# Pre-activation convolution with binarised inputs on one core: fills first, shorter warm-up, both x copies ahead of the signs, and a new order on VectorE

## The reference

```python
mean, std = jnp.mean(W), jnp.sqrt(jnp.var(W))
B = jnp.sign(W[None] - mean + us[:, None, None, None, None] * std)   # 5 sign filters
alpha = jnp.linalg.solve(Bf.T @ Bf, Bf.T @ wf)
W_eff = jnp.einsum('m,mhwio->hwio', alpha, B)
...
for n in range(3):
    An = jnp.sign(jnp.clip(X + v[n], 0.0, 1.0) - 0.5)
    out = out + beta[n] * (conv(An) + sum_alpha * bias[n])
...
x = x + conv_ref(group_norm(x))     # G = 32 groups: one channel each
```

## Time and profile before

| | |
|---|---|
| median of 3 runs | 214.75 us (213.79 to 215.58) |
| profiled execution | 215.01 us |
| its span | 213.2 us |
| busy: PE, DVE, ACT, POOL | 82%, 79%, 66%, 29% |

### The profile page before, as it was taken

One profiled execution on the slowest core, in us unless ns is written; L12 is line 12 of the kernel. 1 busy time (PEld: TensorE's weight loads), 2 busy tenths in 40 slices (PEclk: granted clock), 3 DMA queues, 4 the chain that ended last, 5 costly groups with the idle time before them and its releaser, 6 DMA issues.

```text
span 213.2 us, 4788 instructions
## 1 busy us (share of the span) xinstructions
PE 175.3 (82%) x1812; PEld 132.9 (62%) x1812; DVE 168.5 (79%) x422; ACT 139.9 (66%) x183; POOL 61.4 (29%) x76
## 2 busy tenths in 40 slices
PE   1675128969999999999999999999999998889771
PEld 0574018658777676767777676767676765657451
DVE  4369989478989898989898989888888989874141
ACT  2639157078787878787878787878787878673120
POOL 1279023313223323232323232323232323240000
PEclk9999999979999999999999999999999999999996
DMA  4899123032697978788798879879897455658524
GB/s 117 241 271 272 36 58 101 0 89 70 177 246 221 251 200 233 220 224 261 188 279 238 227 198 267 258 205 246 220 242 221 124 167 144 164 160 226 156 65 151
DMA packets 21030, 39.61 MB, mean 186 GB/s; under 512 B 9744, under 2 KB 9744, under 8 KB 21008
## 3 DMA queue, kind: packets, MB, share of 16 engines
q1 hardware_dynamic: 20272, 39.27, 66.7%
q10 hardware_dynamic: 736, 0.04, 0.2%
HBM read 13.15 MB, written 12.85 MB: 122 GB/s over the span
## 4 chain that ended last, share of the span: by engine, by line
DVE 46%; ACT 21%; issue 13%; PE 11%; DMA 5%; SPq 2%; DVEq 0%; ACTq 0%
DVE y_nat L546 9%; ACT signs L348 8%; DVE s_even L612 8%; DVE raw_stats L555 7%; ACT y_ch L361 6%; ACT x_ch L343 4%; PE conv_ps L722 4%; DVE neg_thr L591 4%; DVE hi_part L601 4%; DVE hi_part L599 4%; DMA x_nat<-in_x 3%; ACT root L353 2%; PE x_ps L684 2%; PE y_ps L757 2%; DVE lane_stats L562 2%
## 5 line engine op out<-in xcount | busy, mean ns | idle before, releaser
L722 PE MATMUL conv_ps<-s_even,w_mm 128*64 128x448 f16 (+1 forms) x576 | 104.7, 336 | 2.4 <-DMA s_odd<-s_even 2.4
L725 PE MATMUL conv_ps<-s_odd,w_mm 128*64 128x448 f16 (+2 forms) x576 | 104.6, 324 | 0.0
L348 ACT ACTIVATE signs<-x_ch,neg_thr 128x784 f16<-128x784 f32 x96 | 85.4, 941 | 20.5 <-DVE neg_thr L591 20.5
L722 PEld LDWEIGHTS conv_ps<-s_even,w_mm 128*64 128x64 f16 x576 | 61.3, 111 | 30.1 <-issue 4.3
L725 PEld LDWEIGHTS conv_ps<-s_odd,w_mm 128*64 128x64 f16 x576 | 61.4, 111 | 0.1
L546 DVE SCALAR_TENSOR_TENSOR y_nat<-y_ps,y_const,x_nat 112x1024 f32<-112x1024 f32 (+1 forms) x32 | 36.6, 1142 | 11.3 <-PE y_ps L742 11.3
L684 PE MATMUL x_ps<-ident,x_nat 112*128 112x112 f32 x224 | 32.1, 291 | 13.2 <-ACT x_ch L343 10.2
L555 DVE BATCH_NORM_STATS2 raw_stats<-x_ch 128x6 f32<-128x448 f32 (+1 forms) x64 | 33.0, 558 | 11.1 <-ACT x_ch L343 11.1
L303 POOL TENSOR_SCALAR lo_part<-signs,ratio_lo 128x1568 f16<-128x1568 f16 x16 | 25.6, 1599 | 56.1 <-ACT signs L348 55.9
L307 POOL TENSOR_SCALAR lo_part<-signs,ratio_lo 128x1568 f16<-128x1568 f16 x16 | 25.1, 1572 | 57.4 <-DVE half_hi L605 53.5
L742 PE MATMUL y_ps<-ident,y_ch 128*112 128x128 f32 x224 | 30.9, 278 | 8.5 <-DVE y_nat L546 7.5
(11 more groups left out here) (106 smaller groups left out, 100.6 us busy)
## 6 DMA issues: line engine op xcount, KB each, us to landing
x_nat<-in_x SPq DMA_DIRECT2D x16, 448.0 KB, 5.3
out<-y_nat SPq DMA_DIRECT2D x16, 448.0 KB, 3.7
s_odd<-s_even SPq DMA_DIRECT2D x32, 203.0 KB, 2.9
s_odd<-s_even SPq DMA_DIRECT2D x32, 188.5 KB, 3.0
x_nat<-in_x SPq DMA_DIRECT2D x16, 336.0 KB, 4.8
out<-y_nat SPq DMA_DIRECT2D x16, 322.0 KB, 2.6
s_odd<-s_even SPq DMA_DIRECT2D x32, 14.5 KB, 2.6
x_nat<-in_x SPq DMA_DIRECT2D x16, 14.0 KB, 5.4
```

The costliest lines, as they stand in the source:

```text
L348: act.activation(signs[q % 2][:, n, :, a, :], x_ch[q % CH_SLOTS][:, :, a, :], ACT.Sign, bias=neg_thr[q % 2][:, n, a:a + 1]).then_inc(signe ...
L722: last = nc.tensor.matmul(low[:, 0:n * ROWS], wt, s_even[b][:, part, r0:r0 + 2 * n, t:t + H], start=first, stop=end)
L725: last = nc.tensor.matmul(high[:, 0:m * ROWS], wt, s_odd[b][:, part, r0:r0 + 2 * m, t:t + H], start=first, stop=end and not at_edge)
```

## The change

Seven edits:

1. POOL fills the padding of `s_even` and `w_edge` before it waits for the filter's load, not between the ratios and its first product.
2. The warm-up matmuls are 4, not 10, and stand ahead of the left x of pair 3 and not behind it.
3. ACT's right copy of pair p+4 stands behind the left copy, ahead of the first two signs of pair p+3. It was the first of the next step. PE's order of transposes is not changed.
4. DVE's high sum stands between the pair moments and the reciprocal.
5. The second residual add of pair p stands in its own step, ahead of the low sum. It was the first of the next step.
6. The right moments and the spread stand behind the left moments, at the end of the step.
7. At the start, the right moments of pair 1 stand ahead of the last two eliminations.

```diff
-WARM = 10
+WARM = 4
 # gpsimd, before the wait for the filter
+            for b in range(S_SLOTS):
+                edge = s_even[b][:].rearrange("p s r h -> p (s r) h")
+                pool.memset(edge[:, :, 0], 0.0).then_inc(pads_ready, 1)
+                pool.memset(edge[:, :, HP - 1], 0.0).then_inc(pads_ready, 1)
+            pool.wait_ge(pads_ready, 2 * S_SLOTS)
+            pool.memset(w_edge[:], 0.0).then_inc(edge_zero, 1)
...
 # scalar, step(p)
-                if real(p + 3):
-                    copy_in(p + 3, 1)
...
                     copy_in(p + LEAD, 0)
+                    copy_in(p + LEAD, 1)
                 if real(p + 3):
                     begin_signs(p + 3)
...
 # vector, step(p)
-                if real(p - 1):
-                    add_x(p - 1, 1)
-                if real(r):
-                    lane_moments(r, 1)
-                    spread_lanes(r)
...
                     pair_moments(r)
-                    n = divide_variance(r, invert_root(r))
                 if real(q):
                     sum_high(q)
                 if real(r):
-                    make_thresholds(r, add_root(n))
+                    make_thresholds(r, add_root(divide_variance(r, invert_root(r))))
+                if real(p):
+                    add_x(p, 1)
                 if real(q):
                     sum_low(q)
...
-                if real(p + LEAD):
-                    lane_moments(p + LEAD, 0)
+                if real(t):
+                    lane_moments(t, 0)
+                    lane_moments(t, 1)
+                    spread_lanes(t)
...
 # tensor, step(p): moved ahead of bring_in(p + LEAD, 0)
+                if p == -1:
+                    pe.wait_ge(hi_made, 1)
+                    for _ in range(WARM):
+                        nc.tensor.matmul(y_ps[:, 1, 0:128], ones[:], ones[:], start=True, stop=True)
```

More of the change, by code:

```diff
@@ L287, in split_ratios @@
                 ts(ratio_lo[:], ratio_lo[:], LO_SCALE, 1.0, ALU.mult, ALU.mult).then_inc(ratios_ready, 1)
+            for b in range(S_SLOTS):
[4 more added lines that the diff above has]
+            pool.memset(w_edge[:], 0.0).then_inc(edge_zero, 1)
+            pool.wait_ge(edge_zero, 1)
             pool.wait_ge(w_loaded, 32)
@@ L293, in _ @@
             pool.wait_ge(ratios_ready, 3)
-            for b in range(S_SLOTS):
-                edge = s_even[b][:].rearrange("p s r h -> p (s r) h")
-                pool.memset(edge[:, :, 0], 0.0).then_inc(pads_ready, 1)
-                pool.memset(edge[:, :, HP - 1], 0.0).then_inc(pads_ready, 1)
             def weigh_low(q):
@@ L311, in _ @@
             pool.wait_ge(w_signed, M_FIL)
-            pool.wait_ge(pads_ready, 2 * S_SLOTS)
             pool.memset(filt[0:C, :, 1, :, 0:M_FIL], 0.0).then_inc(corners_zero, 1)
@@ L315, in _ @@
             pool.wait_ge(corners_zero, 2)
-            pool.memset(w_edge[:], 0.0).then_inc(edge_zero, 1)
-            pool.wait_ge(edge_zero, 1)
             weigh_low(0)
@@ L405, in _ @@
             copy_in(1, 0)
+            copy_in(1, 1)
             begin_signs(0)
@@ L619, in step @@
             def step(p):
-                q, r = p + 2, p + 3
-                if real(p - 1):
-                    add_x(p - 1, 1)
-                if real(r):
-                    lane_moments(r, 1)
-                    spread_lanes(r)
+                q, r, t = p + 2, p + 3, p + LEAD
                 if real(q):
@@ L662, in _ @@
             lane_moments(1, 0)
-            for m in range(2, M_FIL):
-                eliminate(m)
+            eliminate(2)
+            lane_moments(1, 1)
+            spread_lanes(1)
+            eliminate(3)
+            eliminate(4)
             substitute()
@@ L667, in _ @@
             dve.wait_ge(pads_ready, 2 * S_SLOTS)
-            for p in range(-2, PAIRS + 1):
+            for p in range(-2, PAIRS):
                 step(p)
@@ L753, in step @@
                     gather_lanes(p + 3)
-                if p == -1:
-                    pe.wait_ge(hi_made, 1)
-                    for _ in range(WARM):
-                        nc.tensor.matmul(y_ps[:, 1, 0:128], ones[:], ones[:], start=True, stop=True)
                 if real(p + 1):
```

## The result

| | before | after |
|---|---|---|
| median (runs) | 214.27 us (4) | 207.05 us (4) |
| lowest to highest | 213.06 to 215.58 | 205.79 to 209.37 |
| profiled execution / its span | 215.01 / 213.2 | 206.35 / 204.6 |
| ratio after to before | | 0.964, interval 0.955 to 0.974 |

The change makes the kernel 3.6% faster. The forecast was 213.1 us with a range of 210.3 to 216.8; the result lies outside it, near the rival "ring not closed" (207), which had 0.05. But that rival is not what happened.

A forecast was written before the change was run, and what follows sets the result against it. The prediction took a ring of waits between VectorE and ScalarE as the bound. From the 213.2 us span, start -1.5, loop +0.5 and end -0.6 gave 211.6, a median of 213.1 us, range 210.3 to 216.8.

The forecast's parts named there:

- ring not closed: Rival, loop: a term of the new ring overlaps, PE's 10.1 us is the step, 207 us in all; chance 0.05.
- What bounds before: Loop before: a ring of waits between VectorE and ScalarE bounds, not PE; period 10.64 us.
- the old ring: Loop before: ACT's right copy, DVE's moments to thresholds, ACT's signs and scale-out; 10.64 us, DVE waiting 0.36 and 0.50.
- The new ring: Loop after: PE right x transposes, ACT copy, two signs, left scale-out, PE through right out-transposes; 10.68 us per step.
- the sum of the ring's terms: Loop: right x transposes 0.81, copy 0.61, signs 1.70, scale-out 0.99 and 0.15, PE 0.89, 0.97, 0.37, 3.57, 0.67; 10.68 taken.
- The start: Before the loop: first convolution at about 33.9 instead of 38.59; 1.5 us kept, bounds -2.7 to +1.0.
- a low clock: Start: first convolution partly at 1.2 GHz, costing 0 to 3.5 us; the middle, 1.8, was taken.
- GpSimd's blocks: Loop: GpSimd products hold DVE's high sum about 0.35 us and the spread or first weighting about 0.2, within 0.83 slack.
- The rival: Loop: GpSimd's products hold DVE longer, over 0.83 us per step; 216.1 to 221, middle 218.6 us; chance 0.11.
- The end: Last steps: the shift behind the low sum has no store beside it; -0.6 us, bounds -1.5 to +0.9.

The follow-up runs named there:

- the operation inside and outside: Kernel after plus an unread 128x128 ACT copy per step: behind the right copy of x 209.31 us, ratio 0.982; between left and right copies 207.30 us, 0.974.
- Copy back: Kernel after with ACT's right copy of x put back to the start of the next step: period 10.53 us, span 211.4 us, runs too scattered for a ratio.
- fills back: Kernel after with GpSimd's fills put back between the ratios and the first product: 207.17 us, ratio 0.972 to the kernel before.
- no warm-up: Kernel after without any warm-up matmul: 207.79 us, ratio 0.975 to the kernel before.
- four instead of ten: Kernel before with four warm-up matmuls, not ten, in the old place: 212.0 us, ratio 0.993.
- head only: Kernel before with only the fills moved first and four warm-up matmuls ahead of the left x of pair 3: 210.68 us, ratio 0.984.
- Scale-out first: Kernel after with ACT's left scale-out of pair p+1 ahead of the first two signs of pair p+3: 209.65 us, ratio 0.979 to the kernel before.
- add back: Kernel after with the second residual add put back into the next step, behind the spread: 224.15 us, ratio 1.050 to the kernel before.
- right x first: Kernel after with PE's right x transposes ahead of its right out-transposes and DVE's second add behind the low sum: 205.48 us, ratio 0.951; repeated 203.46, 0.953.

## Why the prediction was wrong

**What bounds before** was right. With edit 3 undone the old ring comes back with both its waits, and edit 3 alone removes it.

**The new ring** was right as a mechanism: its order, its closing, the waits of ACT (1.16 us, 1.5 foreseen), PE (0.63 for `y_ch`, 0.7 foreseen) and DVE (0.31 for signs, 0.3 foreseen), and that less waiting on DVE is no time by itself. The rival "ring not closed" is refuted by the operation inside and outside.

**The failed step is the sum of the ring's terms**, 10.68 against 10.34. Link by link, predicted and measured after: 0.81 and 0.78; 0.61 and 0.63; 1.70 and 1.67; scale-out up to PE 1.14 and 1.05; 0.89 and 0.92; left x up to the gather 0.92 and 0.77; gather up to the convolution 0.37 and 0.24; 3.57 and 3.57; 0.67 and 0.70. Of the difference of 0.35 us the two around the gather have 0.28. I had noticed that the gather might wait, and took out 0.05. It had cost more, as the gather's weight load shows. Before, it waited for the spread; after, it ran beside the transposes:

```profile
103.34 0.30 PEld L692 LDWEIGHTS x_ps<-spread_stats,same_ch 128*128 128x128 f32 x2 [0.25 <-DVE spread_stats L565]
```

```profile
98.26 0.30 PEld L693 LDWEIGHTS x_ps<-spread_stats,same_ch 128*128 128x128 f32 x2
```

A better row stood in the trace of before, in the step that follows the start:

```profile
50.25 0.93 PE L684 MATMUL x_ps<-ident,x_nat 112*128 112x112 f32 x8
51.02 0.31 PE L692 MATMUL x_ps<-spread_stats,same_ch 128*128 128x24 f32 x2
```

There the gather follows 0.77 us behind and lasts 0.31, where the earlier trace rows have 0.97 and 0.40. In the earlier trace rows the spread ended at 103.28 (103.10 and 0.18 us) and the gather began at 103.34. In the kernel after the spread ends 0.9 us before the gather. Copy back confirms it: with the old ring the gather waits 0.25 us again and lasts 0.40. My bounds of 10.63 to 10.85 came from the same few rows, so they did not hold the value either. The forecast had the loop 0.5 us longer, and it became 3.6 shorter: 4.1 of the 7.0 us between the span I summed, 211.6, and the measured 204.6. The start has 2.4 of the rest and the end 0.5.

**The start** gained 3.9 us, not 1.5. The first convolution came at 33.52 (33.9 foreseen), but I charged 1.8 us for a low clock that was not there. More than that: most of such a term is not on the path. With slow matmuls in the first convolution (fills back, 4.95 us to the gather and not 3.57) the start is as long as without, and with all of it slow (no warm-up, 6.06 us) it is 0.9 longer. There the convolution took 2.49 us more, and DVE waited 1.00: about 1.5 us are hidden behind DVE, and 1.8 would have cost 0.3 (an estimate from these two figures). The right convolution, at clock 0.50 in the earlier trace rows and foreseen so again, was at 1.00 in the kernel after. That was luck, since in eight of the 16 traces of the experiments a part of it was at 0.50. The head is DVE's once its wait of 2.67 us for the gather of pair 2 is gone, and the edits clear the same wait, so their gains don't add: four instead of ten saves 1.45 us between pairs 1 and 3, edits 1 and 2 2.0, edit 3 alone 2.9, and all together 2.9. The other 1.0 us stands ahead of the root of pair 1 (27.08 and 26.10). It was there in each kernel with edit 1 or edit 7 and in none that had neither, but since starts with the same code differ by up to 1.5 us in the traces (24.73 to 26.21), this is read and not shown.

The Trainium skill says (page "TensorE: Matmul & The Clock Gate", section "What's actually happening") that sustained activity releases the throttle. The runs agree in part: without warm-up the first convolution was slow, and with four it was fast in the kernel after and in seven more traces, but slow in the kernels with the fills back and with the operation outside, whose PE does the same up to there (and in copy back and head only, where PE's left transposes of x came later). So four leave it open which level the convolution gets. None of it told how much of the convolution's time was on the path; that only DVE's rows could have told.

**The edits of DVE:** edit 4 is worth nothing, as predicted; edit 5 too, but beside edit 6 it is needed (without it the kernel is 5% slower than before), which I had priced only as PE's 0.55 us.

**GpSimd's blocks:** 0.27 per step for the high sum (0.35 foreseen), none for the spread (0.2 foreseen). DVE's two weighings start 0.94 us apart and take 0.53 where nothing holds them, so it waits 0.41 of the 10.34 us (the view names 0.31 of it) and needs 9.93: 9.66 of its own (9.85 foreseen) and 0.27 of block. Before blocks the slack was 0.68 us and not 0.83, since the ring was shorter than I had summed. Scale-out first spent it: 9.66 + 0.63 + 0.28 = 10.57, the period measured. The rival was nearer than its price suggested.

**The end** gained 1.1 us (0.6 foreseen), but head only shows it without any edit there.

What stays open: why steps alternate in add back; the other 0.07 of the 0.35 us; why in six of the 18 traces one shift to `s_odd` lands late, so that one step is 0.5 to 1.2 us longer; and why a part of the first right convolution is at clock 0.50 in some traces (with the new ring the step behind it is then 0.5 to 0.8 us longer, or 0.15 with right x first).

## What to carry to other kernels

Where engines run in order and wait for each other, the period is the longest ring of waits; write it down link by link, from start to start, and for each link look whether the instruction that ends it waited for something outside the ring. If it did, take that link from another place of the trace where it didn't: an error of 0.3 us in one link counts as often as the loop runs. An engine whose views name no wait need not be the bound: compare the distance between two of its instructions with that distance where nothing holds it. Before pricing a term at the start, ask which engine is full there; the others' terms are hidden up to the slack behind it, and gains by several edits that clear the same wait do not add.

## What the hardware did that I had not expected

**The block between VectorE and GpSimd goes by who starts first.** I had counted only the case in which VectorE comes later. In the loop the product started at 100.13 and the high sum, begun at 101.27, took 1.25 us. In the start of the kernel after the high sum began first and kept its time, and the product took longer. DVE and POOL there:

```profile
25.99 0.92 DVE L612 TENSOR_TENSOR s_even<-half_hi,signs 128x1568 f16<-128x1568 f16 x1
27.09 1.26 DVE L582 SCALAR_TENSOR_TENSOR twice_dev<-moments,inv_root 128x2 f32<-128x2 f32 x1
```

```profile
26.04 2.30 POOL L310 TENSOR_SCALAR lo_part<-signs,ratio_lo 128x1568 f16<-128x1568 f16 x1 [4.35 <-DVE half_hi L605]
```

The product has 2.30 us instead of 1.57, and a tiny combination behind the high sum is held until it ends (1.26 us instead of 0.16). In both cases the later one waits, whichever engine it is on, and an instruction of 128x2 numbers is held as one of 128x1568 is.

**A small instruction can be the costly one.** The spread of 128x24 numbers takes 0.18 us alone and 0.81, 1.04 and 1.18 us when it starts inside a product (scale-out first, add back, the start of the kernel after). In the first two its lateness reached PE.

**The level that the record of the granted clock does not show.** From 33 to 37 us it is 1.00 in both the kernel after and the one with the fills back. Yet in the first the gather of pair 2 follows the start of the convolution by 3.57 us, and in the second by 4.95, with 0.55 us for its first matmul. The duration of a known matmul told the level there; the clock's record did not.
